# Low halves of the tokens by a matmul with minus the identity, and the bias in the last feature's place

## The reference

```python
x = x + _L0_conv_ref(_ln_c(x), ...)      # 32x32 Fourier modes, 64x64 channels mixed
t = _to_tokens(x)                        # 32768 tokens of 64 features
t = t + _L0_ffn_ref(_ln_t(t), router_w, router_b, expert_w, expert_b)
x = _from_tokens(t, x)
x = x + _L1_conv_ref(_ln_c(x), kernels)  # depthwise, 29x29
t = t + _L1_ffn_ref(_ln_t(t), ...)       # as above, other weights
```

## Time and profile before

| | us |
|---|---|
| median of 3 runs | 941.23 (940.68 to 942.5) |
| profiled execution | 941.57, of which its span 939.8 |
| busy in the span: PE, DVE, POOL, ACT | 807.8, 774.9, 567.3, 545.1 |
| mean granted clock of TensorE | 0.928 of 2.4 GHz |

### The profile page before, as it was taken

The page is one execution under the profiler, slowest core; times in us unless marked ns, Lnnn a source line. Parts: engine busy times, 40 slices in busy tenths (PEclk is TensorE's granted clock), DMA queues, the critical chain, the costliest instruction groups (busy, mean ns, idle before and its releaser), DMA issues.

```text
span 939.8 us, 23972 instructions
## 1 busy us (share of the span) xinstructions
PE 807.8 (86%) x9242; PEld 654.8 (70%) x9242; DVE 774.9 (82%) x1421; ACT 545.1 (58%) x1111; POOL 567.3 (60%) x504
## 2 busy tenths in 40 slices
PE   5996888667999898875899999999848889999987
PEld 5995877634666665543899999999725566666654
DVE  5757688879999999999887677675687999998884
ACT  2467485778787877321444444444268777878621
POOL 2780201247799998896654244340116889999998
PEclk9998576979999999999899999999957999999999
DMA  9988200021887777783787877878100101101111
GB/s 371 369 260 284 70 1 2 2 53 79 321 333 313 317 301 295 291 321 121 260 282 249 283 271 251 284 267 275 42 1 1 46 24 46 46 23 46 47 45 45
DMA packets 48291, 163.06 MB, mean 174 GB/s; under 512 B 9425, under 2 KB 9937, under 8 KB 46033
## 3 DMA queue, kind: packets, MB, share of 16 engines
q1 hardware_dynamic: 48208, 161.96, 47.6%
HBM read 93.46 MB, written 68.49 MB: 172 GB/s over the span
## 4 chain that ended last, share of the span: by engine, by line
PE 32%; POOL 32%; DVE 19%; issue 10%; DMA 3%; ACT 3%; SPq 1%; POOLq 0%; DVEq 0%; ACTq 0%
PE pair L1704 24%; POOL R L573 18%; POOL R L583 11%; DVE R L906 5%; DMA X<-x_rows 3%; PE pair L1498 3%; DVE R L662 3%; DVE R L835 2%; DVE work L662 2%; PE pair L1719 1%; DVE R L846 1%; ACT pair L1251 1%; DVE R L829 1%; PE pair L1629 1%; DVE X L1071 1%
## 5 line engine op out<-in xcount | busy, mean ns | idle before, releaser
L906 DVE TENSOR_TENSOR R<-pair,R 128x896 f32<-128x896 f32 x256 | 275.5, 1082 | 26.7 <-PE pair L1612 26.1
L573 POOL TENSOR_TENSOR R<-R 128x768 f32<-128x768 f32 x128 | 231.9, 1812 | 70.8 <-DVE R L906 70.8
L1704 PE MATMUL pair<-R 128*128 (+4 forms) x2880 | 227.2, 243 | 9.5 <-DVE R L984 9.2
L1704 PEld LDWEIGHTS pair<-R 128*128 128x128 f16 x2880 | 224.2, 98 | 12.8 <-issue 10.3
L1611 PE MATMUL pair<-work,R 128*128 128x448 f16 x512 | 186.5, 364 | 45.1 <-DVE R L906 44.2
L1251 ACT ACTIVATE pair<-X,work 128x64 f32<-128x64 f32 x480 | 166.4, 393 | 57.6 <-DVE R L846 55.2
L1612 PE MATMUL pair<-work,R 128*128 128x448 f16 x512 | 185.5, 362 | 0.0
L583 POOL TENSOR_TENSOR R<-R 128x512 f32<-128x512 f32 x128 | 164.6, 1286 | 10.0
L1373 ACT COPY R<-R 128x1152 f32<-128x1152 f32 x64 | 81.9, 1283 | 117.3 <-PE pair L1704 117.3
L999 DVE COPY R<-R 128x1152 f32<-128x1152 f32 x64 | 94.6, 1479 | 63.7 <-PE pair L1704 63.0
L1629 PE MATMUL pair<-R,ident_sb 128*128 128x256 f32 x496 | 131.3, 388 | 0.6 <-ACT pair L1297 0.4
(11 more groups left out here) (138 smaller groups left out, 1243.2 us busy)
## 6 DMA issues: line engine op xcount, KB each, us to landing
taps_halves<-R SPq DMA_DIRECT2D x128, 458.5 KB, 3.6
R<-taps_halves SPq DMA_DIRECT2D x64, 917.0 KB, 4.7
X<-x_tok SPq DMA_DIRECT2D x4, 2048.0 KB, 17.8
out<-X SPq DMA_DIRECT2D x15, 512.0 KB, 2.7
R<-spec_pairs SPq DMA_DIRECT2D x16, 272.0 KB, 5.2
X<-x_rows SPq DMA_DIRECT2D x4, 1024.0 KB, 11.3
R<-x_chan SPq DMA_DIRECT2D x4, 1024.0 KB, 14.3
X<-x_rows SPq DMA_DIRECT2D x2, 2048.0 KB, 27.4
```

The source lines that it names most:

```text
L573: pool.tensor_tensor(pr[:, :, 192:384], pr[:, :, 0:192], pr[:, :, 192:384], ALU.add).then_inc(half_ready, 1)
L906: dve.tensor_tensor(pr.rearrange("p t (e c) -> p t e c", c=C), pair[p % 2][:, :].rearrange("p (t e c) -> p t e c", t=2, c=C)[:, :, 0:NE - ...
L1704: mm = pe.matmul(acc[:, y0:y1, x0:x1, :], blocks[i % 2][:, ks, 2 - y, 1 - x, :], src[:, y0 + y:y1 + y, x0 + x:x1 + x, :], start=(ks == 0 a ...
```

## The change

- The low half of a block is formed on PE: a matmul of minus the f16 identity with the high half adds to what stands in `xn_psum`, and ACT copies the bank out as f16 (`lower_part` on PE, `take_low` on ACT, both in step `LOW_AT[j]`; on PE it is issued behind the sums and ahead of the pair). This holds for all blocks but the first 11 of each layer (chunk 0, chunk 1 and three of chunk 2), which stay with DVE.
- Since the normalised features add up to zero, the last feature's weights are subtracted from those of the others, and its place (`BIAS`, 63) holds a one that meets the bias. `vh` and its copies and fills go; `u` is multiplied with `wa` and with `wb`. Only 63 features are normalised, copied and subtracted.
- `ident16` becomes identity and minus identity side by side. Four matmuls put bank 5 in the state in which later matmuls add to it. Bank 5 is then used for nothing else: the second bank of the first turns in layer 1 is bank 7, and that of the last sums bank 6.
- The weights are prepared in 6 steps on DVE in place of 7.

The diff, cut to its core:

```diff
-        ident16_sb = sb("ident16_sb", P, F16)
+        ident16_both = sb("ident16_both", 2 * P, F16)
+        ident16_sb, minus_ident16 = ident16_both[:, 0:P], ident16_both[:, P:2 * P]
-        vh = [R3[:, 4096 + 2048 * i:4096 + 2048 * (i + 1)].bitcast(F16) for i in range(2)]
+        BIAS = C - 1
+        LOWERED_FROM = 4 * 2 + LOW_AHEAD
...
+            def bias_columns():                                   # POOL
+                both = R3[:, 10240:12288].bitcast(F16).rearrange("p (t s c) -> p t s c", s=2, c=C)
+                pool.memset(both[:, :, 0, BIAS:C], 1.0)
+                pool.memset(both[:, :, 1, BIAS:C], 0.0).then_inc(ones_ready, 1)
...
-                    pool.memset(vh[q][64:128, :].bitcast(F32), ONES).then_inc(ones_ready, 1)
...
-                    if following and p in LOW_AT[LOW_AHEAD:]:         # DVE, expert_chunk
-                        low_parts(layer, k + 1, LOW_AT.index(p))
-                    if normed and p in LOW_AT[:LOW_AHEAD]:
-                        low_parts(layer, k + 2, LOW_AT.index(p))
...
+            def take_low(layer, k, j):                            # ACT
+                act.wait_ge(lowered, layer * (4 * NCHUNK - LOWERED_FROM) + 4 * k + j - LOWERED_FROM + 1)
+                act.copy(halves_of(j)[:, :, 1, 0:BIAS], tile_columns(xn_psum)).then_inc(tok_low, 1)
...
-                act.copy(u[q][:, at].bitcast(F32), src)
-                act.copy(vh[q][0:64, at].bitcast(F32), src[0:64]).then_inc(parts_copied, 1)
+                act.copy(u[q][:, at].bitcast(F32), src).then_inc(parts_copied, 1)
...
+                    if following and p in LOW_AT[LOW_AHEAD:]:         # ACT, behind normalise, ahead of copy_parts
+                        take_low(layer, k + 1, LOW_AT.index(p))
+                    if normed and p in LOW_AT[:LOW_AHEAD]:
+                        take_low(layer, k + 2, LOW_AT.index(p))
...
+            for i in range(4):                                    # PE, ahead of the inverse transform
+                pe.matmul(xn_psum[:, i * P:(i + 1) * P], ident16_sb, ident16_sb, start=(i == 0), stop=(i == 3),
+                          skip_group_check=True)
...
-                    mm = pe.matmul(dst, vh[q][:, t * P:(t + 1) * P], wb[:, 0:EW], start=False, stop=True)
+                    mm = pe.matmul(dst, u[q][:, t * P:(t + 1) * P], wb[:, 0:EW], start=False, stop=True)
...
+            def lower_part(layer, k, j):                          # PE
+                n = (layer * NCHUNK + k) * 4 + j
+                pe.wait_ge(tok_high, n + 1)
+                pe.matmul(tile_columns(xn_psum), minus_ident16, halves_of(j)[:, :, 0, 0:BIAS], start=False, stop=True,
+                          skip_group_check=True).then_inc(lowered, 1)
...
                         sum_quad(layer, k if g >= 0 else k - 1, q if g >= 0 else 1 - q, g % NQUAD)
+                    if following and p in LOW_AT[LOW_AHEAD:]:
+                        lower_part(layer, k + 1, LOW_AT.index(p))
+                    if normed and p in LOW_AT[:LOW_AHEAD]:
+                        lower_part(layer, k + 2, LOW_AT.index(p))
                     expert_pair(layer, k, q, p)
```

More of the change, by code:

```diff
@@ L216, in metaformer @@
         tok_low = sem("tok_low")
+        lowered = sem("lowered")
         parts_copied = sem("parts_copied")
@@ L349, in low_columns, with tile_columns, halves_of @@
                     xf1[:, 0, bo, :, w0:w0 + 4])
+        def tile_columns(tile):
+            return tile.rearrange("p (t c) -> p t c", c=C)[:, :, 0:BIAS]
+        def halves_of(j):
+            return parts[j].rearrange("p (t s c) -> p t s c", s=2, c=C)
         block = ctx.enter_context(nc.Block())
@@ L630, in _ @@
                 if layer:
[L631 to L635, removed]
-                    pool.memset(vh[q][64:128, :].bitcast(F32), ONES).then_inc(ones_ready, 1)
-                    pool.wait_ge(ones_ready, 2 * layer + q + 1)
-                if layer:
+                    pool.wait_ge(convolved, C)
+                    bias_columns()
                     pool.wait_ge(conv_copied, C)
@@ L1277, in copy_parts @@
                     act.wait_ge(summed, (layer * NCHUNK + k - 2) * NOCT + j + 1)
-                src = bank[4 + j % 2] if layer and k == 0 else bank[4]
+                src = bank[4 + 3 * (j % 2)] if layer and k == 0 else bank[4]
                 at = slice(8 * j * P, 8 * (j + 1) * P)
-                act.copy(u[q][:, at].bitcast(F32), src)
-                act.copy(vh[q][0:64, at].bitcast(F32), src[0:64]).then_inc(parts_copied, 1)
+                act.copy(u[q][:, at].bitcast(F32), src).then_inc(parts_copied, 1)
             def exp_second(layer, k):
@@ L1306, in copy_last @@
                     act.wait_ge(summed, (layer + 1) * NCHUNK * NOCT)
-                    act.mul(X[:, at:at + 256], bank[5][:, 0:256], 1.0 / SCALE).then_inc(sum_copied, 1)
+                    act.mul(X[:, at:at + 256], bank[6][:, 0:256], 1.0 / SCALE).then_inc(sum_copied, 1)
             def early_seed():
@@ L1582, in turn_tokens @@
                 n = (layer * NCHUNK + k) * 4 + j
+                if k == 0 and j == 0:
+                    pe.wait_ge(ones_ready, layer + 1)
                 pe.wait_ge(tok_low, n + 1)
@@ L1586, in turn_tokens @@
                     pe.wait_ge(parts_copied, n - 1 if start else n)
-                out_ = bank[4 + j % 2 if start else 4].bitcast(F16)
+                out_ = bank[4 + 3 * (j % 2) if start else 4].bitcast(F16)
                 for t in range(8):
-                    mm = pe.transpose(out_[:, t * P:(t + 1) * P], parts[j][:, t * P:(t + 1) * P], ident16_sb[:, :])
+                    mm = pe.transpose(out_[:, t * P:(t + 1) * P], parts[j][:, t * P:(t + 1) * P], ident16_sb)
                 mm.then_inc(across, 1)
@@ L1599, in route @@
                     pe.matmul(dst, u[q][:, t * P:(t + 1) * P], wa[:, EC:EC + NE], start=True, stop=False)
-                    mm = pe.matmul(dst, vh[q][:, t * P:(t + 1) * P], wb[:, EC:EC + NE], start=False, stop=True)
+                    mm = pe.matmul(dst, u[q][:, t * P:(t + 1) * P], wb[:, EC:EC + NE], start=False, stop=True)
                 if j == 3:
                     mm.then_inc(logits_ready, 1)
+            def lower_part(layer, k, j):
[3 more added lines that the diff above has]
+                          skip_group_check=True).then_inc(lowered, 1)
             def expert_pair(layer, k, q, p):
@@ L1635, in sum_quad @@
                               skip_group_check=True)
-                    mm = pe.matmul(dst, vh[q][:, t * P:(t + 1) * P], wb[:, EW:EC], start=False, stop=(t % 4 == 3),
+                    mm = pe.matmul(dst, u[q][:, t * P:(t + 1) * P], wb[:, EW:EC], start=False, stop=(t % 4 == 3),
                                    skip_group_check=True)
@@ L1645, in sum_last @@
                 for i in range(2):
-                    dst = bank[7 - 2 * i]
+                    dst = bank[7 - i]
                     w = quarter[(2 * NOCT - 2 + i) % 8].rearrange("p (t j c) -> p t j c", t=4, c=C)
@@ L1652, in sum_last @@
                         pe.matmul(dst[:, C * t:C * (t + 1)], u[1][:, at:at + P], wa[:, EW:EC], start=False, stop=False)
-                        pe.matmul(dst[:, C * t:C * (t + 1)], vh[1][:, at:at + P], wb[:, EW:EC], start=False, stop=False)
+                        pe.matmul(dst[:, C * t:C * (t + 1)], u[1][:, at:at + P], wb[:, EW:EC], start=False, stop=False)
                     pe.wait_ge(quarter_ready, 2 * n + 1 + i)
@@ L1758, in expert_layout @@
     b = np.concatenate([np.asarray(expert_b).reshape(-1), router_b])
-    low = np.zeros((64, m.shape[1]), np.float32)
-    low[0] = low[32] = b
-    return np.ascontiguousarray(np.concatenate([np.concatenate([m, m], 0), np.concatenate([m, low], 0)], 1))
+    rows = np.concatenate([m[:C - 1], b[None]])
+    last = np.concatenate([np.repeat(m[C - 1:], C - 1, 0), np.zeros_like(b)[None]])
+    return np.ascontiguousarray(np.tile(np.concatenate([rows, last], 1), (2, 1)))
 def host_layout(x, L0_conv_kernel_base, ffn0, ffn1, kernels):
```

52 lines of the change are left out of this document (25 added, 27 removed).

## The result

The change made the kernel slower: 966.18 us (963.69 to 969.43, 4 runs) against 941.87 us for the kernel before, a ratio of 1.026 (95% interval 1.0225 to 1.0294), +24.3 us where +22.5 was forecast. The profiled execution, 963.69 us, is the lowest of the four; its span is 961.9 us against 939.8.

The account below looks back on a forecast made before the run. A ring between PE and ACT bounds chunks 1 to 5 at 31.0 us each: +11.2 + 13.4 - 0.6 - 1.4 - 0.4 + 0.3 = +22.5 us, on the median 963.7, told as 964; range 951 to 973 us.

Parts of the forecast that it names:

- chunks 1 to 5, layer 0: Overlapped chunks of layer 0's expert stage: 31.0 us each, 155.0 us for five where they took 143.84, +11.2.
- chunks 1 to 5, layer 1: Overlapped chunks of layer 1's expert stage: 31.0 us each, 155.0 us for five where they took 141.61, +13.4.
- chunk 6, 7 and the passage to the convolution, layer 0: End of layer 0's expert stage: one block left in chunk 6, one DVE slot won there, -0.6 us.
- up to and in chunk 0 of both layers: Stage starts: second copy gone -1.4 us, weight cast gone -0.4, four matmuls preparing the bank +0.3.
- chunks 6 and 7, layer 1: End of layer 1's expert stage: chunk 6 has one block left, nothing counted.
- The ring: PE's sum releases ACT, ACT's high half PE's matmul, then the next sum: 7.40 us, 7.88 with a router part.
- the gate's share: In step 11 ACT waits for DVE's gate, which needs pair 10: 0.45 us more per chunk.
- The wait: PE idle in chunks 1 to 5 for ACT's high half, 0.5 to 1.5 us before pairs 2, 6, 10, 14.
- One sign: Chunk 5 of layer 1 (26.76 us) should grow by about 4 us, else the ring is mis-summed.
- The first rival, POOL taking over: DVE's relief ends POOL's waits in chunks 1 to 5: -23.3, 916 us, or 927 with half ended; chance 0.07.
- the starts: Starts of both expert stages lose the second copy where it is on the chain: -1.4 us in all.
- DVE's one slot in chunk 6 of layer 0: DVE, 28.17 busy of 28.53 us, sets that chunk and wins one subtraction slot, -0.6 us.

Follow-up runs that it names:

- E7: Subtraction on DVE, rest of the change kept; PE only waits for the high half ahead of pairs 2, 6, 10, 14, no matmul or low-half copy: 968.77 us.
- E2: Changed kernel with the new matmul on PE and ACT's low-half copy one step later, behind that step's sums: 926.04 us, ratio 0.982 to before.
- E1: Changed kernel with the low half's subtraction back on DVE in all blocks, all else of the change kept: 935.38 us, ratio 0.9923 to before.
- E5: Changed kernel with the new matmul in its same step on PE, but behind the pair: 941.10 us, ratio 0.998 to before.
- E6: Changed kernel with both the matmul and low-half copy one step later and ACT's high half ahead of taking out the sum: 942.11 us, ratio 1.0001.
- E4: Changed kernel with the new matmul one step earlier, on PE alone (ahead of pairs 1, 5, 9, 13): 1067.72 us, ratio 1.133 to before.
- E3: Changed kernel with ACT's order alone turned, high half ahead of taking out the sum in steps 1, 5, 9, 13: 933.07 us, ratio 0.9894.

## Why the prediction was right

| step of the prediction | forecast us | measured us |
|---|---|---|
| chunks 1 to 5, layer 0 | +11.2 | +12.4 |
| chunks 1 to 5, layer 1 | +13.4 | +13.0 |
| chunk 6, 7 and the passage to the convolution, layer 0 | -0.6 | 0.0 |
| up to and in chunk 0 of both layers | -1.5 | -4.9 |
| chunks 6 and 7, layer 1 | 0 | +1.5 |
| span | +22.5 | +22.1 |

The table is of the profiled executions; between the medians the change costs 24.3 us.

The mechanism held at each step. The ring's lengths come from rows of the kernel before (3.30 us of ACT with both hand-overs, 4.10 or 4.58 of PE) and were met within 0.05 us but for the gate's share (0.32 for 0.45). The wait is where it was forecast, of about the size forecast (0.56 to 1.65 us for 0.5 to 1.5), and E7 shows that a wait there suffices for such a loss. One sign came out smaller: chunk 5 of layer 1 grew by 3.4 us (26.76 to 30.14), not by about 4.

The first rival, POOL taking over, did not have its condition met in the change. E2 meets it, and shows that its price was too high: 9.5 us in the ten chunks and not 23.3. The prediction took all of POOL's waits for gain (13.1 and 10.2 us) and so put POOL's own chunk at 26.1 us. But of the 13.1 only 4.1 lie in chunks 2 to 4, and 9.0 in chunks 1 and 5, where 7.2 of them are left in E2; and a chunk in which POOL waits 0.2 us still takes 26.91.

The Trainium skill's page "Perfetto Trace Analysis" (Optimizing Scalar/DVE Operations) says that handing work from a saturated DVE to ScalarE may pay. The runs agree in E2, where the hand-over gains 9 us on E1 (926.04 and 935.38), and not in the change, where it loses 31 (966.18); what decides here is where the receiving queues wait.

Four terms were mis-sized, and they cancel in part. The first is the starts, which gained 4.9 us and not 1.5: up to POOL's first addition -1.4 in layer 0 (198.72 to 197.35) and -0.8 in layer 1, and in chunk 0 -1.4 (38.91 to 37.51) and -1.3. In layer 0 E1 has the same 37.51 for that chunk (197.20 to 234.71), so there the gain belongs to the removed second copy and its companions, and not to the matmul; I had counted only the copies that the chain named. In layer 1 E1's chunk 0 takes 36.21 us (before 36.77, the change 35.47), at a granted clock of 0.83 (0.82 and 0.88), so the cause of the gain there stays open. Which of the companions gave how much was not tried.

The second term takes chunk 0's gain back: chunk 1 grew by 1.3 us in layer 0, from 30.62 to 31.90, where the forecast's 31.0 left it 0.4. Chunks 0 and 1 of layer 0 together take 69.53 us before and 69.41 after, so the row of the starts and that of the chunks should be read together. Third, DVE's one slot in chunk 6 of layer 0 did not show (30.23 us before, 30.29 after); the 28.53 us from which the prediction took it end at 410.00, 1.7 us ahead of POOL's first addition of chunk 7. Fourth, chunk 6 of layer 1 grew by 1.5 us (26.64 to 28.14), where nothing was counted. The ring reaches into its step 2; it is 26.33 in E1 and 26.68 in E2, which fits, but no run moves that block alone.

In E1 to E5 and E7 the direction was as the ring has it, but only E2 lay inside the time expected, and E6 went against it. The rows put the differences down to a second constraint each time: the clock (E4), the gate (E3, E5), DVE's subtraction (E7), the seed (E6). None of these was changed by itself.

## What to carry to other kernels

Before work is moved to another engine's queue, mark the row of before at which its input was ready and the row at which the new queue will want it; if the input is late there, and its maker waits for something behind the new place in that queue, add up the ring by slots: it bounds the period, however idle the engines are. The cure is a place and not less work: a step later gave 40 us here with the same instructions. And look for every ring that the new order closes: a cure on each side (E6) closed one that neither cure has alone.

## What the runs showed that I had not expected

- A wait of 2.55 us in PE's queue can be followed by matmuls at the lower clock level: E4's rows at 325.34 to 328.1 (0.37 us apart in place of 0.19), clock 0.88 over the chunk. Another wait of the same length 10 us later was not. Waits up to 2.20 us in chunks 1 to 5 of the change left 1.00.
- The added matmul of 504 columns was 0.39 us long and had a slot of 0.23 (304.83 to 305.06, the next pair's first matmul), as taken from the 448-column one.
- A wait that does no work (E7) cost as much as the wait with all the work behind it, 968.8 and 966.2 us, though DVE's subtraction had a part in E7's rings.
